# Folding three weight-load stages around LayerNorm and the V projection into their neighbours, in an eight-core macaron transformer layer

## What is computed

```python
x = x + 0.5 * ffn(layernorm(x), U1, V1, b1, U2, V2, b2)
x = x + attn(layernorm(x), Q_w, Q_b, K_w, K_b, V_w, V_b, O_w, O_b)
x = x + 0.5 * ffn(layernorm(x), U1, V1, b1, U2, V2, b2)
# ffn:  P = y @ U1 (1024 -> 256); H = gelu(P @ V1 + b1) (-> 4096); Q = H @ U2 (-> 256); Q @ V2 + b2
# attn: 16 heads of 64, q,k,v = y @ W + b, causal softmax(q k^T / 8) v, then @ O_w + O_b
# layernorm: (x - mean) / sqrt(var + 1e-5), no scale or shift
```

## Time and profile before

| | us |
|---|---|
| median of 2 runs | 2079.44 |
| the profiled execution | 2091.66 |
| its slowest core (core 7), first to last instruction | 2090.1 |
| first feed-forward with its statistics | 32 to 366 |
| Q and K weight load for pair 0 | 366 to 379 |
| statistics and V weight load | 379 to 429 |
| row arithmetic and `yb2` | 429 to 466 |
| V weight sum, V bias, `vaug` | 466 to 479.6 |
| V block | 479.6 to 592 |
| memsets, Q and K weight load for pair 1 | 592 to 608.5 |
| attention pairs | 608.5 to about 1622 |
| output projection, second feed-forward, store | about 1622 to 2090 |

### The profile page before, as it was taken

How to read it: one execution, slowest core, us unless ns; L and a number is a source line. 1 busy time by engine, 2 the same in 40 slices (tenths; PEclk the granted TensorE clock), 3 DMA queues, 4 the chain that set the end, 5 groups by cost and what they waited for, 6 DMA issues and landing times. The chain is left out here.

```text
span 2090.1 us, 17713 instructions; the slowest of 8 cores (2031.3 to 2090.1 us)
## 1 busy us (share of the span) xinstructions
PE 1559.5 (75%) x5640; PEld 418.0 (20%) x5640; DVE 566.8 (27%) x911; ACT 554.7 (27%) x609; POOL 96.2 (5%) x108
## 2 busy tenths in 40 slices
PE   2189998328939979698796978969798493499994
PEld 0022222002312212121121211212111130122220
DVE  3322211452511412314133141322401235410211
ACT  1222222010003333333333343333343002222220
POOL 0100000000000100000010000100000001000000
PEclk9589997757865757668586775867555697588986
DMA  7400000200040010200102011010000205000003
GB/s 237 126 1 0 1 1 1 70 30 26 33 93 1 11 41 1 51 1 11 41 1 51 1 28 24 11 31 1 21 0 1 81 1 189 13 0 1 0 1 161
DMA packets 63653, 72.68 MB, mean 35 GB/s; under 512 B 20390, under 2 KB 51254, under 8 KB 61516
## 3 DMA queue, kind: packets, MB, share of 16 engines
q1 hardware_dynamic: 63564, 71.54, 11.7%
HBM read 50.49 MB, written 12.58 MB: 30 GB/s over the span
## 5 line engine op out<-in xcount | busy, mean ns | idle before, releaser
L686 ACT ACTIVATE pt<-p_big 128x1024 bf16<-128x1024 f32 (+3 forms) x320 | 286.5, 895 | 598.8 <-PE p_big L647 339.3
L641 PE MATMUL p_big<-qgA,kgA 65*128 65x512 bf16 (+3 forms) x320 | 151.0, 472 | 134.0 <-ACT pt L686 61.7
L531 ACT ACTIVATE hb<-p_big 128x1024 bf16<-128x1024 f32 x128 | 131.0, 1024 | 311.0 <-PE p_big L454 306.3
L452 PE MATMUL p_big<-pb,v1b 128*128 128x512 bf16 x512 | 162.1, 400 | 11.8 <-DVE pb L489 11.8
L600 PE MATMUL p_big<-pt,v_pair 128*64 128x512 bf16 (+3 forms) x320 | 159.6, 499 | 0.0
L603 PE MATMUL p_big<-pt,v_pair 128*64 128x512 bf16 (+3 forms) x320 | 158.8, 496 | 0.0
L647 PE MATMUL p_big<-qgB,kgB 65*128 65x512 bf16 (+3 forms) x320 | 157.5, 492 | 0.0
L596 PE MATMUL p_big<-pt,ones_bf 128*1 128x512 bf16 (+3 forms) x320 | 156.4, 489 | 0.0
L592 PE MATMUL p_big<-pt,ones_bf 128*1 128x512 bf16 (+3 forms) x320 | 147.1, 460 | 0.2
L462 PE MATMUL p_big<-hb,u2b 128*128 128x512 bf16 x512 | 140.4, 399 | 3.4 <-ACT hb L531 3.4
L454 PE MATMUL p_big<-r_ones,r_b 1*128 1x512 bf16 x256 | 102.5, 400 | 0.0
(11 more groups left out here) (142 smaller groups left out, 1609.3 us busy)
## 6 DMA issues: line engine op xcount, KB each, us to landing
wstage<-u SPq DMA_DIRECT2D x40, 256.0 KB, 4.3
wstage<-v SPq DMA_DIRECT2D x40, 256.0 KB, 4.0
x<-xT SPq DMA_DIRECT2D x8, 1024.0 KB
outT<-x SPq DMA_DIRECT2D x8, 1024.0 KB, 11.0
wst<-qw SPq DMA_DIRECT2D x8, 512.0 KB
wst<-kw SPq DMA_DIRECT2D x8, 512.0 KB
wstage<-vw SPq DMA_DIRECT2D x16, 256.0 KB
vscr<-vb_s SPq DMA_DIRECT2D x32, 128.0 KB
```

Source lines behind the costliest of these rows:

```text
L452: tensor.matmul(psl, v1b[:, rc, 128 * fc:128 * (fc + 1)], pb[:, c % 2, rc, :], start=(rc == 0), stop=False)
L531: ACT.inc(scalar.activation(hb[:, 2 * (fp % 2):2 * (fp % 2) + 2, :], psl.rearrange("p (a b) -> p a b", a=2), AF.Gelu_apprx_tanh))
L641: mm = tensor.matmul(p_big[:, 0:w], kgA[:, ksl], qgA[:, lo:hi], start=True, stop=not first)
L686: ch["XA"].inc(scalar.activation(pt[:, :, i % 2, 0:w], p_big[:, 0:1024].rearrange("p (a b) -> p a b", a=2)[:, :, 0:w], AF.Exp))
```

## The change

- **Statistics, all three times.** `xb_s` shrinks from two buffers of 2048 columns to two of 1024. DVE casts half a chunk (1024 columns), squares it in two pieces, and goes on; TensorE waits per half.
- **Head pair 0.** The block `emit_qk_weight_loadcast(0)` goes. Its loads are appended to `extra_loads` of attention's statistics: behind the 16 V pieces come four pieces each of the Q and K weight (128 KB, 256 elements per partition) and four bias pieces (0.5, 0.5, 2 and 2 KB), 28 in all.
- **V bias and V weight sum.** Their blocks go. The bias is two of those pieces. The 16 matmuls of the sum stand ahead of group 0 in the V block, in `p_big`, and TensorE waits there for DVE's copy (position 0.2).
- **The hand-written order in the V block.** `ws` two groups later; `pj` t ahead of group 10 + t, `pjev` t at 10.6 + t; `nrm` two groups later, 17 to 22; `red` i at 19.0 + i; `prod` at 27.0 and `urow` at 27.5.
- **Head pair 1.** The block `emit_qk_weight_loadcast(1)` goes. SP loads Q at the start of the V block; DVE casts it at position 28.0. SP, after the store of group 24, waits for that cast, loads K, and DVE casts it at 29.5, behind `vev(29)`. After the store of group 30 SP loads the two bias rows, cast at 31.8.

```diff
@@ emit_ln_stats
-                xb_s = mk(lctx, "xb_s", [128, 2, S], BF16)
+                xb_s = mk(lctx, "xb_s", [128, 2, 1024], BF16)
@@ DVE
+                            for half in range(2):
+                                hs = 2 * c + half
+                                if hs >= 2:
+                                    vector.wait_ge(PE.h, pe0 + 4 * (hs - 1))
+                                cc = CAST.inc(vector.tensor_copy(
+                                    xb_s[:, hs % 2, :], x[:, c, 1024 * half:1024 * (half + 1)]))
+                                vector.wait_ge(CAST.h, cc)
+                                for jj in range(2):
+                                    t = 4 * c + 2 * half + jj
+                                    sl = slice(512 * jj, 512 * (jj + 1))
+                                    if t >= 2:
+                                        vector.wait_ge(PE.h, pe0 + 2 * t - 2)
@@ emit_attn_sublayer
-                emit_qk_weight_loadcast(0, ct)
...
+                           + [(srcq0[:, 2 * i:2 * i + 2, :],
+                               ct["wqb"][:, 2 * i:2 * i + 2, :], 0.125) for i in range(4)]
+                           + [(srck0[:, 2 * i:2 * i + 2, :],
+                               ct["wkb"][:, 2 * i:2 * i + 2, :], None) for i in range(4)]
+                           + [(din["qb"].ap()[0:1, 0:128], ct["r_qkb"][0:1, 0:128], 0.125),
+                              (din["kb"].ap()[0:1, 0:128], ct["r_qkb"][0:1, 128:256], None),
+                              (din["vb"].ap()[0:1, 0:512], r_scv[0:1, 0:512], None),
+                              (din["vb"].ap()[0:1, 512:1024], r_scv[0:1, 512:1024], None)])
+                    emit_ln_stats(r_rstd, r_mr, extra_loads=wl2, stage=wstage0)
...
-                    emit_wsum_row(vaug_r[0:1, 0:D], lambda c: wb[:, c, :], NC, D)
-                    load_stage(wstage0, [(din["vb"].ap(), r_sc[0:1, 0:D])])
@@ V block
+                        def vwsum_pe(tensor):
+                            mm = None
+                            for c in range(NC):
+                                for jj in (0, 512):
+                                    mm = tensor.matmul(p_big[0:1, jj:jj + 512], neg_bf[:, :],
+                                                       wb[:, c, jj:jj + 512],
+                                                       start=(c == 0), stop=(c == NC - 1),
+                                                       skip_group_check=True)
+                            PE.inc(mm)
+                            tensor.wait_ge(EV.h, ev_vw)
+
+                        g_sched = {0: [vwsum_pe]}
                         for st, fn in aux0["pe_sched"]:
-                            gk = min(31, max(0, int((st - 3) * 0.7)))
+                            if 16 <= st <= 23:
+                                gk = 10 + (st - 16)
+                            else:
+                                gk = min(31, max(2, int((st - 3) * 0.7) + 2))
...
-                                dvepl.append((6.8 + t, lambda v, t=t: aux0["dve_pjev"](v, t)))
+                                dvepl.append((10.6 + t,
+                                              lambda v, t=t: aux0["dve_pjev"](v, t)))
...
-                                dvepl.append((16.0 + i, lambda v, wh=wh, j=j:
+                                dvepl.append((19.0 + i, lambda v, wh=wh, j=j:
...
+                            def lc_cast_q(v):
+                                v.wait_ge(ch["PJ"].h, aux0["pj0"] + 10)
+                                v.wait_ge(LD.h, ld_lc + 16)
+                                ROW.inc(v.tensor_scalar(ct["wqb"][:, :, :], stvd, 0.125,
+                                                        None, OP.mult))
...
+                            dvepl.append((28.0, lc_cast_q))
+                            dvepl.append((29.5, lc_cast_k))
+                            dvepl.append((31.8, lc_cast_b))
@@ SP in the V block, after the store of group g
+                                    if g == 24:
+                                        sync.wait_ge(ROW.h, row_lc + 1)
+                                        LD.inc(sync.dma_start(
+                                            stv, din["kw"].ap()
+                                            .rearrange("(c p) m -> p c m", p=128)
+                                            [:, :, 128:256]), 16)
+                                    if g == 30:
+                                        sync.wait_ge(ROW.h, row_lc + 2)
+                                        LD.inc(sync.dma_start(
+                                            ct["wst4"][0:1, 0, 0, 0:128],
+                                            din["qb"].ap()[0:1, 128:256]), 16)
...
-                emit_qk_weight_loadcast(1, ct)
```

More of the change, by code:

```diff
@@ L204, in _ @@
                         for c in range(NC):
[L205 to L215, removed]
+                            for half in range(2):
[10 more added lines that the diff above has]
+                                        vector.wait_ge(PE.h, pe0 + 2 * t - 2)
+                                    ROW.inc(vector.tensor_tensor(
+                                        sq_s[:, t % 2, :], xb_s[:, hs % 2, sl],
+                                        xb_s[:, hs % 2, sl], OP.mult))
                         for i in range(nw):
@@ L228, in _ @@
                         for c in range(NC):
-                            tensor.wait_ge(CAST.h, cast0 + c + 1)
                             for j in range(4):
                                 t = 4 * c + j
+                                hs = 2 * c + j // 2
                                 sl = slice(512 * j, 512 * (j + 1))
-                                PE.inc(tensor.matmul(p_big[0:1, sl], ones_bf[:, :], xb_s[:, c % 2, sl],
+                                ssl = slice(512 * (j % 2), 512 * (j % 2 + 1))
+                                tensor.wait_ge(CAST.h, cast0 + hs + 1)
+                                PE.inc(tensor.matmul(p_big[0:1, sl], ones_bf[:, :],
+                                                     xb_s[:, hs % 2, ssl],
                                                      start=(c == 0), stop=(c == NC - 1)))
@@ L1086, in emit_attn_sublayer @@
                     r_rstd = mk(rctx, "r_rstd2", [1, S])
[L1087 to L1092, removed]
+                    srcq0 = din["qw"].ap().rearrange("(c p) m -> p c m", p=128)[:, :, 0:128]
+                    srck0 = din["kw"].ap().rearrange("(c p) m -> p c m", p=128)[:, :, 0:128]
+                    wl2 = ([(din["vw"].ap().rearrange("(c p) m -> p c m", p=128)
+                             [:, c:c + 1, 512 * h:512 * (h + 1)],
+                             wb[:, c:c + 1, 512 * h:512 * (h + 1)], None)
+                            for c in range(NC) for h in range(2)]
+                           + [(srcq0[:, 2 * i:2 * i + 2, :],
[7 more added lines that the diff above has]
+                    emit_ln_stats(r_rstd, r_mr, extra_loads=wl2, stage=wstage0)
                     with nc.Block() as blk:
@@ L1186, in _, with vwsum_ev @@
                                     dvepl.append((g + 0.5, vev))
[L1187 to L1188 removed]
+                            def vwsum_ev(v):
+                                v.wait_ge(PE.h, pe0 + 1)
+                                v.wait_ge(LD.h, ld_vb)
+                                EV.inc(v.tensor_copy(vaug_r[0:1, 0:D], p_big[0:1, 0:1024]))
+                            dvepl.append((0.2, vwsum_ev))
@@ new lines, in lc_cast_k, with lc_cast_b @@
+                            def lc_cast_k(v):
+                                v.wait_ge(LD.h, ld_lc + 32)
+                                ROW.inc(v.tensor_copy(ct["wkb"][:, :, :], stvd))
+                            def lc_cast_b(v):
+                                v.wait_ge(LD.h, ld_lc + 64)
+                                ROW.inc(v.tensor_scalar(ct["r_qkb"][0:1, 0:128],
+                                                        ct["wst4"][0:1, 0, 0, 0:128],
+                                                        0.125, None, OP.mult))
+                                ROW.inc(v.tensor_copy(ct["r_qkb"][0:1, 128:256],
+                                                      ct["wst4"][0:1, 0, 1, 0:128]))
```

31 lines of the change are left out of this document (22 added, 9 removed).

## The result

The changed kernel takes 2093.24 us (median of 27 runs, 2083.6 to 2111.23), the kernel before 2078.93 (26 runs). The ratio is 1.009, 95% interval 1.0066 to 1.0114, so 14 to 24 us slower, with 18.7 in the middle: clear of noise, inside 2%, and inside the range of 2060 to 2107. (The ratio leaves out the executions in which one die of the chip ran at a lower clock than the other, so 18.7 is not the 14.3 between the two medians.) Four blocks are gone from the program and it is slower.

The account below looks back on a forecast made before the run. It took the bound to change from stage to stage: DMA waits, DVE's statistics loop, load-and-cast chains, TensorE in the V block. Terms -12.5 + 15.2 + 0.5 - 2.75 - 2.5 + 16.9 - 10.8 gave +4, 2083.5 us; 8-in-10 range 2060 to 2107.

Parts of the forecast that it names:

- Parts 1 and 2: Before and in attention's statistics: pair 0's block goes, -12.5 us; its loads return as a chain behind the statistics, +15.2.
- Part 3: All three statistics stages: half-chunk casts add instructions and a wait but free buffers sooner, +0.5 us, bounds -2 and +8.
- Part 4: V weight sum and bias moved ahead of group 0: -2.75 us; TensorE warmer for groups 0 and 1: -2.5.
- Part 5: Order inside the V block: TensorE waits for projection evictions, +10.5 us, and for red calls, +6.4; +16.9 in all.
- the branch I called likeliest, at 2083.5: Whole kernel: the forecast as summed, a change of -8 to +10 us, chance 0.62.
- one of my own signs of being wrong: V block: the forecast is wrong if 8 matmuls in groups 18 to 31 take 3.4 us.
- the rival at 2094: V block, groups 18 to 22: TensorE's clock falls in the nrm stretch, +8.5 us, +11 with slow groups behind; chance 0.17.
- My argument from the statistics' row: V block's nrm stretch: its share of busy time lies between the statistics, at clock 1.00, and yb2, at 0.50.
- Part 6: End of the V block: pair 1's block goes, -12.7 us; its tail stays, +1.9; -10.8, bounds -12.7 and -8.
- The sum: Whole kernel: all terms together +4 us, giving 2083.5 us from the median of 2079.4.
- most of the rivals: V block: waits don't come, 2066, chance 0.15; short clock fall, 2094, 0.17; long fall, 2135, 0.04; SP's wait stalls evictions, 2088.
- The bound of "faster by over 2% isn't in these edits": Whole kernel: even with parts 2, 3 and 5 at zero the sum is -28.5 us, 1.4%; over 2% faster, chance 0.03.

Follow-up runs that it names:

- e7: Changed kernel with head pair 0's weight block put back and its ten pieces out of the statistics' list; the two stretches 14.7 and 51.6 us, against 2.7 + 64.0.
- e6: Kernel before with the half-chunk casts alone; one profile, attention's statistics stage 49.3 us instead of 51.0.
- e1: Changed kernel with projection evictions, red, prod and urow placed earlier in the V block's order; 2067.54 us, ratio 0.9946 to the kernel before.
- e2: Kernel before with only the changed hand-written order of the V block; 2099.48 us, ratio 1.0104.
- e9: Changed kernel with ten unread matmuls ahead of the nrm of groups 20, 21 and 22; one profile, stretch to the last V matmul 127.1 us instead of 130.5.
- e10: e5 with pair 1's Q cast at position 24.6 and K cast at 28.2; 1999.98 us, ratio 0.9583 to the kernel before.
- e5: Changed kernel with the repairs of e1 and e3, and the feed-forwards' weight casts on ACT and POOL, none on DVE; 2000.61 us, ratio 0.9594 to the kernel before.
- e3: Changed kernel with all 28 pieces in attention's statistics cast by ACT through four slots; 2057.4 us, ratio 0.9887 to the kernel before.

## Right and wrong, by the prediction's steps

- **Parts 1 and 2 were right in mechanism and size.** -12.1 for -12.5. The 12 pieces took 14.9 us where I had 15.2 (a 128 KB pair 2.8 for 2.75, the bias pairs 1.8 on average for 2.1). e7 shows the exchange directly.
- **Part 3: wrong in sign, on a small term.** I had +0.5; DVE's loop became 1.5 us shorter in attention, and only attention's stage passes that on (e6). The step that was off is the length of a half: I had 1.64 us and it takes 1.54, sixteen times. The fixed cost per instruction that the Trainium skill's "VectorE: DVE Perf Modes" gives in its section on the TRN2 errata is there in the rows, and larger: 2 x 0.69 - 1.22 = 0.16 us for each added cast, where its 58 cycles would be 0.06. It was more than paid by waits that vanished, so a loss is not what the runs show.
- **Part 4: right.** 9.6 removed for 10.55, 8.24 added for 7.8 (486.51 - 478.27 on core 0). Groups 0 and 1 start warm, with 1.9 us for eight matmuls, and e1's stretch (102.4 + 8.2 - 1.9 for the two old waits - 105.8) puts that at 2.9 for my 2.5.
- **Part 5: the waits were right, the term was too small.** Seven waits of 1.6 for 1.55, one of 1.3, `nrm` 8.3 for 8.2: 17.3 us more than before, where I had 16.9. What the step left out of the sum was the clock, which it had as a rival with a chance of 0.17 and a price of 8.5 to 11 (five groups at 1.65 are 8.25). It did fall, on all eight cores of every kernel with this order, but for at most three groups, 20 to 22, and mostly for parts of them. At the full clock these three would take 5.9 (e2's three cores), 5.6 and 5.8 us (the same 2.75 from the `nrm` to the group's end behind waits of 2.89 and 3.01), 17.3 together; a typical core takes 7.4, 7.0 and 7.0, so the clock cost some 4 us, and 6 on core 7. With it the order costs 24.2 (e2), where I had 16.9; the remaining 2 to 3 us are not assigned. So the branch I called likeliest, at 2083.5, was not the one that came, and one of my own signs of being wrong showed: 8 matmuls at 3.4 us or more in groups 18 to 31, which core 7 has with 3.59. The mechanism of the rival at 2094 is what came. That its number is near 2093.24 is luck: it had too much for the clock and nothing for attention. The Trainium skill, "TensorE: Matmul & The Clock Gate", section on HAM oscillation, has idle gaps send the array back to its slow clock. The trace agrees that idling did it, and e9 that filling the gaps undoes it; but here it happened at gaps of 2.4 to 3.0 us between groups of 2.4, shorter than those that the page names, and not on every core at the first of them, and the measurement decides. No fall came in the first half, where the waits were 1.6 us between 4.6 us of work. My argument from the statistics' row was poor evidence: TensorE has no idle gap over 0.8 us there, so its share of busy time says nothing of gaps of 2.8.
- **Part 6: half right.** The block's 12.7 went, as 12.2. For its tail I had +1.9 and it was +3.3; the memsets came 6.3 us after the last matmul, not 4 to 5. I had K landed and cast 1 us after the last matmul. The load took 5.3 us to land where I had 4.2 from a load that was alone in the queue, and the K cast stood behind `vev(29)`, which waited for the store of group 25, issued behind the load. The K cast ended 3.2 us after the last matmul on core 0 (2.0 to 2.5 on the others), and all that follows shifted. e1's order takes 2.0 us off the tail and e10 the rest.
- **The sum.** +4 forecast; +10.5 in the edited stretches; +18.7 in the whole. The range held, but it is 47 us wide and takes in no change at all and most of the rivals; the middle was 15 us off, 6.5 of them in the edited stretches, where the V block alone was 5.9 over, and 8 that are open. The 1127 us at a clock of 0.69 that the prediction gives for the attention pairs are those of the window from 620 to 1747, which runs on past the output projection; the pairs alone take 1013.5 us on that core, at 0.67. The bound of "faster by over 2% isn't in these edits" held for the edits as made. It said nothing of what lies one line beside them: e5 is 4% faster with the same parts.

## What to carry to other kernels

Where lists are ordered by hand, an operation's place relative to the work that its result releases counts, not its distance from it: an eviction sorted one place behind that of the next group cost 1.6 us every time here, and moving it one place forward cost nothing. When a load is moved out of a block of its own, look at what stands ahead of its cast on the casting engine and how many slots its queue has; a block removed there may only change its name. And 2.4 to 3 idle microseconds between short groups cost a second time here, through TensorE's clock.

## What the hardware showed that I had not expected

TensorE kept the 2.4 GHz level through seven periods of 4.6 us of work and 1.6 of waiting, and lost it right where the waits became 2.4 to 3.0 us, for parts of two or three groups and on some cores for nearly all of them. Ten useless matmuls in each wait made the stretch 3.4 us shorter. With four slots and an idle ACT, 28 loads of 0.5 to 256 KB, 5.2 MB in all, came in within 30 us beside a loop of 25, on eight cores at once (e3), where two slots and DVE needed 64 us. And the attention pairs, equal instructions on every core, took from 982 to 1018 us, in step with the clock that they were granted.
